# Second stage of a four-layer convolution chain: three quantities move from VectorE to ScalarE, and layer three's wraps move ahead of layer two's conversion

## The reference

```
x = x + _L0_conv_ref(_gn(x), 5)      # Newton-Schulz matrix inverse, 5 iterations, per channel
x = x + _L1_conv_ref(_gn(x), ...)    # 3x3 convolution on activations quantised to 8 bit
x = x + _L2_conv_ref(_gn(x), ...)    # 5 taps on a diagonal, zero padding
x = x + _L3_conv_ref(_gn(x), ...)    # 3x3 convolution by FFT: it wraps around the borders

# layer 1, with n = 127:
scale_input = max(abs(x)) / 128
x_q = round(clip(x / scale_input, -n, n))
out = conv(x_q, weight_int8) * (scale_input * scale_weight) + bias
```

## Time and profile before

| | |
|---|---|
| median of 3 runs | 4088.38 us (4086.21 to 4093.47) |
| profiled execution, its own time | 4097.41 us |
| its span in the trace | 4095.5 us |
| mean granted TensorE clock | 0.985 |
| busy over the span: PE, DVE, ACT, POOL | 95%, 85%, 50%, 59% |
| busy from 2630 to 3990 us: PE, DVE, ACT, POOL | 94%, 91%, 26%, 31% |

### The profile page before, as it was taken

How to read it: one execution, slowest core, us unless ns; L and a number is a source line. 1 busy time by engine, 2 the same in 40 slices (tenths; PEclk the granted TensorE clock), 3 DMA queues, 4 the chain that set the end, 5 groups by cost and what they waited for, 6 DMA issues and landing times. The chain is left out here.

```text
span 4095.5 us, 91001 instructions
## 1 busy us (share of the span) xinstructions
PE 3893.8 (95%) x35017; PEld 2998.8 (73%) x35017; DVE 3467.1 (85%) x7396; ACT 2056.7 (50%) x4298; POOL 2417.1 (59%) x3154
## 2 busy tenths in 40 slices
PE   7999999999999999999999499999999999999998
PEld 7999999999999999999999244444444444444443
DVE  5888888888888888888887798999999999999985
ACT  5776777777777777777776122222222222222221
POOL 6888888888888888888887223223322332333222
PEclk9999999999999999999999699999999999999999
DMA  2212222222111222222211476777777777777774
GB/s 72 62 55 62 63 63 63 63 63 63 61 59 59 63 63 63 63 63 63 61 58 40 99 156 153 166 159 159 159 171 162 160 165 162 163 161 162 163 150 107
DMA packets 339917, 422.11 MB, mean 103 GB/s; under 512 B 25312, under 2 KB 288160, under 8 KB 323104
## 3 DMA queue, kind: packets, MB, share of 16 engines
q1 hardware_dynamic: 311840, 342.85, 33.7%
q10 hardware_dynamic: 27648, 73.43, 8.3%
HBM read 135.18 MB, written 134.22 MB: 66 GB/s over the span
## 5 line engine op out<-in xcount | busy, mean ns | idle before, releaser
L1222 POOL TENSOR_TENSOR xn<-F,xn 128x512 f16<-128x512 f32 x512 | 541.7, 1091 | 1245.9 <-ACT xn L1253 1245.9
L1428 PE MATMUL bank<-xn,wt 128*128 128x512 f16 (+1 forms) x3072 | 779.7, 390 | 15.3 <-DVE xn L1299 12.8
L483 ACT ACTIVATE P<-bank 128x512 f32<-128x512 f32 x1024 | 606.3, 607 | 267.1 <-PE bank L1003 155.3
L1450 PE MATMUL bank<-xk,wt 128*32 128x512 f16 x6144 | 633.9, 385 | 4.3 <-DMA xk<-xn 4.3
L1428 PEld LDWEIGHTS bank<-xn,wt 128*128 128x128 f16 (+1 forms) x3072 | 299.8, 104 | 371.1 <-issue 56.0
L1253 ACT ACTIVATE xn<-F 128x2048 f16<-128x2048 f32 x128 | 244.8, 1912 | 611.1 <-DVE F L1368 611.1
L1455 PE MATMUL bank<-xk,wth 128*32 128x512 f16 x3072 | 468.7, 380 | 0.0
L1313 DVE SCALAR_TENSOR_TENSOR x<-bank,wu,x 128x512 f32<-128x512 f32 x512 | 374.0, 742 | 75.0 <-PE bank L1455 49.9
L1450 PEld LDWEIGHTS bank<-xk,wt 128*32 128x32 f16 x6144 | 295.9, 95 | 161.8 <-DMA xk<-xn 4.4
L1433 PE MATMUL bank<-xh,wth 96*128 96x512 f16 (+1 forms) x1024 | 311.6, 386 | 100.2 <-DMA xh<-xn 100.2
L333 POOL TENSOR_TENSOR W<-W 128x512 f16<-128x512 f32 x256 | 289.5, 1164 | 145.0 <-ACT W L516 145.0
(11 more groups left out here) (143 smaller groups left out, 8458.4 us busy)
## 6 DMA issues: line engine op xcount, KB each, us to landing
X<-in_x SPq DMA_DIRECT2D x64, 1024.0 KB, 4.8
x_scratch<-X SPq DMA_DIRECT2D x64, 1024.0 KB, 5.5
X<-x_scratch SPq DMA_DIRECT2D x64, 1024.0 KB, 8.3
out<-x SPq DMA_DIRECT2D x64, 1024.0 KB, 4.0
xk<-xn SPq DMA_DIRECT2D x256, 131.8 KB, 6.4
xk<-xn ACTq DMA_DIRECT2D x256, 131.8 KB, 6.2
xh<-xn SPq DMA_DIRECT2D x192, 131.8 KB, 4.4
xh<-xn ACTq DMA_DIRECT2D x192, 131.8 KB, 5.4
```

Source lines behind the costliest of these rows:

```text
L483: nc.scalar.activation(into[:, 4 * q:4 * q + 4, :], banks[q][:, :].rearrange("p (m w) -> p m w", m=4), ACT.Copy).then_inc(sb, 1)
L1222: ins = nc.gpsimd.tensor_tensor(padded(xn[l][n % 2], 1)[:, a + 1:a + 5, L:L + H], F[l][:, a:a + 4, :], padded(xn[l][n % 2], 0)[:, a + 1:a ...
L1428: nc.tensor.matmul(bank, wt[l][:, a, k, :], v, start=(k == a == b == 0), stop=False)
L1450: nc.tensor.matmul(bank[32 * q:32 * q + 32, :], wt[2][:, a, e, 32 * q:32 * q + 32], rows(b, 2 * q + e, 0), start=(a == b == e == 0), stop= ...
```

## The change

The quotient of the quantising, `(x - mean) * a`, is computed by ACT as `a * x + ncol`, where `ncol = -mean * a` is a new column set once before the stage. The same is done for layer 2's scaling to `F` (`ON_ACT = (2,)`), with a column `nb` that DVE computes; layer 3's scaling stays on DVE. On DVE quantising falls into `clamp` and `integers`, and `normalise(3)` stands between them. Two column products of `normalise` become one, and the others are written with column operands in place of tensor ones. In ACT's program the wraps and the halo DMAs of layer 3 now stand ahead of `upper(2)`, and the quotient stands behind the skew DMAs.

```
--- before.py
+++ after.py
@@ -104,6 +104,7 @@
         mcol = persistent("mcol", [H, B])
         acol = persistent("acol", [H, B])
         sws = persistent("sws", [H, 1])
+        ncol = persistent("ncol", [H, B])
         banks = [keep.enter_context(nc.psum_tensor(f"bank{n}", [H, 512], f32)) for n in range(8)]
 
 
@@ -885,6 +886,9 @@
                     link.wait()
                     link.done(nc.vector.tensor_scalar(acol[:, :], acol[:, :], inv[:, 0:1], None, ALU.mult))
                     link.wait()
+                    link.done(nc.vector.scalar_tensor_tensor(out=ncol[:, :], in0=mcol[:, :], scalar=-1.0, in1=acol[:, :],
+                                                             op0=ALU.mult, op1=ALU.mult))
+                    link.wait()
                     dve.wait_ge(pads_zeroed, 6)
                     dve.wait_ge(unscale_ready, 2)
 
@@ -1119,7 +1123,7 @@
             bst_ = [None, None] + [sb(f"bs{l}", [H, BPI, 6]) for l in (2, 3)]
             dev = [None, None] + [sb(f"dv{l}", [H, 2 * BPI]) for l in (2, 3)]
             PART = 512 // 2
-            cols = [None, None] + [{k: sb(f"{k}{l}", [H, 1]) for k in ("m", "s", "q", "ve", "sd", "ra", "rb", "r")}
+            cols = [None, None] + [{k: sb(f"{k}{l}", [H, 1]) for k in ("m", "s", "q", "ve", "sd", "ra", "rb", "r", "nb")}
                                    for l in (2, 3)]
 
             def padded(t, part):
...
@@ -1145,10 +1151,11 @@
             LATE = (None, 0, 1, 3)
+            ON_ACT = (2,)
             STEPS = B + LATE[3]
 
             def there(i):
@@ -1247,8 +1254,20 @@
                         nc.scalar.activation(v[:, :, 0, :], v[:, :, NJ, :], ACT.Copy).then_inc(wrapped, 1)
                         nc.scalar.activation(v[:, :, NJ + 1, :], v[:, :, 1, :], ACT.Copy).then_inc(wrapped, 1)
 
+                    def quotients(n):
+
+                        act.wait_ge(x1_in[n % 2], 16 * (n // 2) + 16)
+                        need(act, normed[1], n)
+                        nc.scalar.activation(T[:, :, :], xs_of(1, n)[:, :, :], ACT.Identity, scale=acol[:, n:n + 1],
+                                             bias=ncol[:, n:n + 1]).then_inc(quotient, 1)
+
                     def upper(l, n):
 
+                        if l in ON_ACT:
+                            act.wait_ge(scale_set[l], n + 1)
+                            need(act, normed[l], n)
+                            nc.scalar.activation(F[l][:, :, :], xs_of(l, n)[:, :, :], ACT.Identity, scale=cols[l]["r"][:, 0:1],
+                                                 bias=cols[l]["nb"][:, 0:1]).then_inc(scaled_f[l], 1)
                         act.wait_ge(scaled_f[l], n + 1)
                         nc.scalar.activation(padded(xn[l][n % 2], 0)[:, 1:NJ + 1, L:L + H], F[l][:, :, :],
                                              ACT.Copy).then_inc(high[l], 1)
@@ -1265,6 +1284,7 @@
                         nc.scalar.activation(xs_of(1, n)[:, :, :], xs_of(1, n)[:, :, :], ACT.Identity,
                                              bias=bst[:, 0:1]).then_inc(biased, 1)
 
+                    quotients(0)
                     first(0)
                     act.wait_ge(xk_zeroed, 2)
                     for s in range(STEPS):
@@ -1272,6 +1292,8 @@
                             act.wait_ge(normed[2], s)
                             for r in range(1, RB, 2):
                                 skew_row(act, r, s - 1)
+                        if there(s + 1):
+                            quotients(s + 1)
                         if there(s - 2):
                             root(3, s - 2)
                             upper(3, s - 2)
@@ -1279,23 +1301,23 @@
                             first(s + 1)
                         if there(s):
                             root(2, s)
-                            upper(2, s)
                         if there(s - 2):
                             wrap(s - 2)
                             act.wait_ge(wrapped, 2 * (s - 1))
                             halo_copies(act, 3, s - 2, True)
+                        if there(s):
+                            upper(2, s)
 
                 @block.vector
                 def _(dve):
-                    def quantise(n):
-
-                        dve.wait_ge(x1_in[n % 2], 16 * (n // 2) + 16)
-                        link = Link(dve, q_chain, 2 * n)
-                        link.done(nc.vector.tensor_scalar(T[:, :, :], xs_of(1, n)[:, :, :], mcol[:, n:n + 1],
-                                                          acol[:, n:n + 1], ALU.subtract, ALU.mult))
-                        link.wait()
-                        link.done(nc.vector.tensor_scalar(T[:, :, :], T[:, :, :], QMAX, MAGIC, ALU.min, ALU.add))
-                        link.wait()
+                    def clamp(n):
+
+                        dve.wait_ge(quotient, n + 1)
+                        nc.vector.tensor_scalar(T[:, :, :], T[:, :, :], QMAX, MAGIC, ALU.min, ALU.add).then_inc(clamped, 1)
+
+                    def integers(n):
+
+                        dve.wait_ge(clamped, n + 1)
                         nc.vector.tensor_scalar(padded(xn[1][n % 2], 0)[:, 1:NJ + 1, L:L + H], T[:, :, :], MAGIC, -QMAX,
                                                 ALU.subtract, ALU.max).then_inc(normed[1], 1)
 
@@ -1356,19 +1378,23 @@
                         dve.wait_ge(groot[l], n + 1)
                         link.done(nc.vector.reciprocal(c["ra"][:, :], c["sd"][:, :]))
                         link.wait()
-                        link.done(nc.vector.tensor_tensor(c["rb"][:, :], c["ra"][:, :], c["ra"][:, :], ALU.mult))
-                        link.wait()
-                        link.done(nc.vector.tensor_tensor(c["rb"][:, :], c["rb"][:, :], c["ve"][:, :], ALU.mult))
+                        link.done(nc.vector.tensor_scalar(c["rb"][:, :], c["ra"][:, :], c["ra"][:, 0:1], c["ve"][:, 0:1],
+                                                          ALU.mult, ALU.mult))
                         link.wait()
                         link.done(nc.vector.tensor_scalar(c["rb"][:, :], c["rb"][:, :], -0.5 * XUP, 1.5 * XUP, ALU.mult, ALU.add))
                         link.wait()
-                        link.done(nc.vector.tensor_tensor(c["r"][:, :], c["ra"][:, :], c["rb"][:, :], ALU.mult))
-                        link.wait()
-                        need(dve, normed[l], n)
-                        nc.vector.tensor_scalar(F[l][:, :, :], xs_of(l, n)[:, :, :], c["m"][:, 0:1], c["r"][:, 0:1],
-                                                ALU.subtract, ALU.mult).then_inc(scaled_f[l], 1)
-
-                    quantise(0)
+                        link.done(nc.vector.tensor_scalar(c["r"][:, :], c["ra"][:, :], c["rb"][:, 0:1], None, ALU.mult))
+                        link.wait()
+                        if l in ON_ACT:
+                            nc.vector.tensor_scalar(c["nb"][:, :], c["r"][:, :], c["m"][:, 0:1], -1.0, ALU.mult,
+                                                    ALU.mult).then_inc(scale_set[l], 1)
+                        else:
+                            need(dve, normed[l], n)
+                            nc.vector.tensor_scalar(F[l][:, :, :], xs_of(l, n)[:, :, :], c["m"][:, 0:1], c["r"][:, 0:1],
+                                                    ALU.subtract, ALU.mult).then_inc(scaled_f[l], 1)
+
+                    clamp(0)
+                    integers(0)
                     for s in range(STEPS):
                         for u in range(BPI):
                             if u == BPI - 1 and there(s - 2):
@@ -1381,9 +1407,11 @@
                         if there(s - 2):
                             variance(3, s - 2)
                         if there(s + 1):
-                            quantise(s + 1)
+                            clamp(s + 1)
                         if there(s - 2):
                             normalise(3, s - 2)
+                        if there(s + 1):
+                            integers(s + 1)
                         for u in range(BPI):
                             if there(s - 3):
                                 residual(3, s - 3, u)
```

More of the change, by code:

```diff
@@ L1130, in conv_net @@
             out_stored = [sem(f"out_stored{n}") for n in range(THIRD)]
-            q_chain = sem("q_chain")
+            clamped = sem("clamped")
+            quotient = sem("quotient")
+            scale_set = [None, None] + [sem(f"scale_set{l}") for l in (2, 3)]
             biased = sem("biased")
@@ L1248, in wrap, with quotients @@
                         nc.scalar.activation(v[:, :, NJ + 1, :], v[:, :, 1, :], ACT.Copy).then_inc(wrapped, 1)
-                    def upper(l, n):
+                    def quotients(n):
+                        act.wait_ge(x1_in[n % 2], 16 * (n // 2) + 16)
+                        need(act, normed[1], n)
+                        nc.scalar.activation(T[:, :, :], xs_of(1, n)[:, :, :], ACT.Identity, scale=acol[:, n:n + 1],
+                                             bias=ncol[:, n:n + 1]).then_inc(quotient, 1)
+                    def upper(l, n):
```

(5 more changed lines are left out.)

12 lines of the change are left out of this document (7 added, 5 removed).

## The result

| | before | changed |
|---|---|---|
| median | 4089.86 us (4086.21 to 4093.47, 4 runs) | 4218.36 us (4216.27 to 4221.23, 4 runs) |
| ratio, 95% interval | | 1.0315 (1.0302 to 1.0328) |
| span of the profiled execution | 4095.5 us | 4218.3 us |

The change makes the kernel 3.15% slower. The prediction said 4218 us. The medians differ by 128.5 us, the two profiled executions by 122.8: the one of the kernel before took 4097.41 us, 7.6 above its median, that of the changed kernel 4220.11 us, 1.8 above.

The account below looks back on a forecast made before the run. The prediction took a closed chain through ACT to bound the changed kernel: terms of 29.1 us plus 0.4 for the store, 29.5 a step against 27.42, giving 4227 us profiled and a median of 4218, range 4130 to 4315.

Parts of the forecast that it names:

- The chain: Second stage: a closed round through ACT, DVE, POOL and DMA issues, 29.1 us, 29.5 with the store, sets every step.
- Skew issue: ACT after POOL's layer 2 pass: four skew DMA issues take 4.3 us, the nearly empty-queue time, instead of 5.16.
- Quotient and scaling: The two operations moved to ACT, the quantising quotient and layer 2's scaling to F, take 2.1 us each.
- Clamp to conversion: DVE's clamp, four small operations and layer 3's scaling, until ACT starts the conversion: 3.29 us together.
- term 4: Layer 3's conversion 1.99 us and POOL 4.23; small halo issue, bias addition and root hide beside POOL with 1 us spare.
- The store's term: Finished image's 1 MB store overlaps ACT's halo issue: nothing at best, 1.9 us at worst, 0.4 us taken.
- The sum: 61 steps of 29.5 instead of 27.42 us add 127 us, the stage's start about 3: 4227 us profiled, 4218 median.
- this rival: PE's clock falls through new waits of 4 us each step; at 0.80 the step is 31.7 us, 4353 us; chance 0.07.
- the limit of 0.86: Mean PE clock above which PE's 25.36 us of work still fit in the 29.5 us step.
- The stretched halo issue: Store stretches ACT's halo issue by 1.9 us: step 31.0 us, 4311 us; decides from a 4.5 us issue; chance 0.13.
- The fast rival: Shorter ACT issues cut the chain to 25.7 us, PE becomes the bound: step 26.0 us, 4000 us; chance 0.09.
- the one of no change: Intermediate ACT issue times let the shorter halo wait and longer chain cancel: step 27.4 us, 4088 us; chance 0.05.

Follow-up runs that it names:

- e6: Changed kernel with four more unused statistics operations on DVE, 2.8 us a step, between the reads of layer 2's banks: 4223.06 us, ratio 1.0314.
- e2: Kernel before with only the wraps and layer 3's halo issue moved ahead of layer 2's conversion: 4052.06 us, ratio 0.9901.
- e4: Changed kernel with the quotient back on DVE ahead of the clamp: 4098.69 us, ratio 1.0017.
- e5: Changed kernel with only ACT's quotient moved ahead of the skew issues: 4038.28 us, ratio 0.9862.
- e9: Changed kernel with ACT's four skew issues given to SP, which then issues all eight: 4015.51 us, ratio 0.9804.

## Why the prediction was right

**The chain.** Its terms, against the changed kernel's own rows. The timelines of ACT, POOL and DVE there:

```profile
3001.99 3.49 ACTq L1185 DMA_DIRECT2D xh<-xn  x3
3005.58 2.10 ACT L1269 ACTIVATE F<-x,nb,r 128x2048 f32<-128x2048 f32 x1 [3.62 <-issue]
3007.71 1.91 ACT L1272 ACTIVATE xn<-F 128x2048 f16<-128x2048 f32 x1
3013.96 4.23 ACTq L1177 DMA_DIRECT2D xk<-xn  x4
3018.30 2.09 ACT L1261 ACTIVATE T<-X,ncol,acol 128x2048 f32<-128x2048 f32 x1 [8.67 <-issue]
```

```profile
3009.70 4.23 POOL L1229 TENSOR_TENSOR xn<-F,xn 128x512 f16<-128x512 f32 x4 [9.04 <-ACT xn L1272]
```

```profile
3021.57 0.16 DVE L1379 RECIPROCAL ra<-sd 128x1 f32<-128x1 f32 x1
3021.76 0.27 DVE L1381 TENSOR_SCALAR rb<-ra,ve 128x1 f32<-128x1 f32 x1
...
3026.03 0.97 DVE L1363 SCALAR_TENSOR_TENSOR dv<-bs,dv 128x8 f32<-128x8 f32 x1
```

Skew issue: 4.3 said, 4.23 measured; the choice of the empty-queue row over the 5.16 of the earlier trace rows was right. Quotient and scaling: 2.1 said, 2.09 and 2.10. POOL twice 4.23. Clamp to conversion: 3.29 said, 3.46 measured (3020.43 to 3023.89): the four small operations take 0.94 us together (3021.57 to 3022.51) and not 0.77, the one with two column operands 0.27, the one with none 0.15 (at 3022.07). POOL ends at 3009.70 + 4.23 = 3013.93, and the skew issue starts at 3013.96, as said. The thin cover of term 4 held as well: ACT waits 0.87 us a step for POOL before the wraps (39.8 in 46), where 1 was said.

**The store's term.** 0.4 us said; the halo issue took 3.42 to 3.49 instead of 3.36, so this is at most about 0.1. No run shows that it comes from the store. What filled the sum up instead were the slower column operations (0.2) and about 0.1 us each between the end of the two long issue bursts and the ACT operation behind them (3018.19 to 3018.30), where 0.03 was said. The step came out at 29.44 for 29.5: a little luck in the small terms, none in the large ones.

**The sum.** The stage's start and end together cost 0.1 us, not 3, and the steps 122.7, not 127: the prediction had 4227 us for a profiled execution, and it took 4220.11. That the median was met to 0.4 us is luck. The 9 us between profiled execution and median, read from the kernel before, are 1.8 in the changed kernel, and this error took the other two back. What was right is the mechanism and the length of the step within 0.1 us.

**What is late besides.** The halo wait went, as said, and PE's wait for layer 2's variance came. It is about 2.4 us a step and not 4, with 0.3 for layer 3's beside it, and PE's own work became longer: 26.8 us a step busy (1233.47 in 46.1 steps) for 25.7 before (1279.43 in 49.8). The clock fell: 0.96 granted in the steady part for 0.99 before. The timeline of PE in the changed kernel shows a wait, slow matmuls, and the same group of six at the usual pace 4 us later:

```profile
3027.24 0.38 PE L1495 MATMUL bank<-q,gm 128*128 128x1 f32 x2 [1.84 <-DVE q L1367]
...
3030.00 1.08 PE L1478 MATMUL bank<-xk,wt 128*32 128x512 f16 x6
...
3034.46 0.62 PE L1478 MATMUL bank<-xk,wt 128*32 128x512 f16 x6
```

and the busy times of the engines around it, columns as in the earlier trace rows, show the granted clock, third column from the end:

```profile
3028.00:3032.00 4.00, 4.00 (x38) 1.66 (x32) 2.28 (x9) 2.50 (x6) 2.11 (x3) 0.57 0.56 231
3032.00:3039.00 7.00, 7.00 (x98) 3.46 (x96) 4.30 (x6) 4.01 (x2) 0.00 (x0) 1.00 0.71 145
```

The clock was 0.57 for these 4 us, near the lower of its two levels, and 1.00 on both sides (from 3015 to 3028 us too). Read in slices of 2 us, it fell like this in 26 of the 46 steps. The Trainium skill (TensorE: Matmul & The Clock Gate, HAM oscillation) says of a loop that waits for data in every iteration that the clock is back at half each time. The trace agrees in the step shown, but not in every step: the clock fell in about every second one. So the mechanism of this rival was there; but PE had the room for it: 0.96 is above the limit of 0.86, and PE is not in the chain. DVE's deviations beside POOL took 0.97 us in this step, as the prediction allowed for.

**The rivals.** The stretched halo issue did not come: it was to decide from 4.5 us on, and 3.49 is the longest of the rows above. The fast rival and the one of no change needed short issues; they kept their 1.06 and 1.16 us each. DVE as a bound was refuted by e6; it is busy 21.7 us a step (1000.99 in 46.1 steps), 21 said.

## What to carry to other kernels

An engine that looks 30% busy may have no room: add its DMA issues and the other engines' work that it waits for, in the order of its program, and ask whether that round closes within one step. Then ask it again of the other engines: once ACT's round was short enough, one through PE and DVE was the bound (e2, e4). Before moving work to an idle engine, place it where that engine waits anyway (e5: the same instructions, 180 us less). And an exchange of two blocks on one engine is judged by what of another engine each one covers; here the exchange took the cover from POOL's 4.2 us.

## What the runs showed of the hardware that I had not expected

Eight skew DMAs issued by SP alone took 5.48 us (0.69 each, in e9), while four by SP and four by ACT at the same time took 3.76 and 4.23 us (0.94 and 1.06 each, in the changed kernel). Issuing from two engines at once saved 1.3 us to the last issue, and cost ACT 4.2 us. That the two slow each other down is what these numbers suggest; issues by ACT alone were not measured.

A one-column operation on DVE with two column operands took 0.27 us, with one 0.21 to 0.22, with immediates 0.15 (changed kernel, 3021.76 to 3022.48).
